# Two copies of the dt rows, and the dt projections in pairs on different row groups

## What is computed

```python
xz = xseq @ in_proj_w.T                 # 384 -> 2 x 768
xin, z = jnp.split(xz, 2, axis=-1)
u = silu(depthwise_conv(xin, taps=3) + conv_b)
dbc = u @ x_proj_w.T                    # 768 -> 24 (dt) + 16 (B) + 16 (C)
dt, Bm, Cm = dbc[..., :24], dbc[..., 24:40], dbc[..., 40:]
dt = softplus(dt @ dt_proj_w.T + dt_proj_b)   # 24 -> 768
A = -exp(A_log)                         # 768 x 16
# for each position t, 768 channels x 16 states:
h = exp(dt_t[..., None] * A) * h + (dt_t * u_t)[..., None] * B_t
y_t = sum_n(h * C_t)
y = (y + u * D) * silu(z)
return y @ out_proj_w.T
```

## Time and profile before

| | |
|---|---|
| Time, median of 3 runs | 3674.62 us (3673.96 to 3679.95) |
| Profiled execution, first to last instruction | 3674.1 us, 50128 instructions |
| Mixer | from 0 to about 2600 us, 16 chunks |
| Two chunks in the steady part | 328 us |
| TensorE's granted clock, mean | 0.969 of full speed |
| DMA, share of the span | 18.6% on the main queue |

### The profile page before, as it was taken

One profiled execution on the slowest core, in us unless ns is written; L12 is line 12 of the kernel. 1 busy time (PEld: TensorE's weight loads), 2 busy tenths in 40 slices (PEclk: granted clock), 3 DMA queues, 4 the chain that ended last, 5 costly groups with the idle time before them and its releaser, 6 DMA issues. The chain is left out here.

```text
span 3674.1 us, 50128 instructions
## 1 busy us (share of the span) xinstructions
PE 3352.4 (91%) x16962; PEld 2370.5 (65%) x16962; DVE 3256.0 (89%) x3376; ACT 2759.3 (75%) x5350; POOL 2577.3 (70%) x2045
## 2 busy tenths in 40 slices
PE   6989989899999989899989989898889998889997
PEld 3666666666666666666666666666657776557776
DVE  3999999999999999999999999999967887876886
ACT  5888797888789788977978787888655554875553
POOL 3898988989898988989898988989921111551100
PEclk7999999999999999999999999999999999999998
DMA  3020211202020211202020210202111113641212
GB/s 134 10 92 19 92 38 65 85 18 85 19 92 19 92 47 55 84 18 85 19 98 23 83 69 33 84 19 85 63 58 35 53 53 143 236 184 40 70 36 87
DMA packets 83586, 249.89 MB, mean 68 GB/s; under 512 B 15212, under 2 KB 24044, under 8 KB 73092
## 3 DMA queue, kind: packets, MB, share of 16 engines
q1 hardware_dynamic: 82564, 245.65, 18.6%
q10 hardware_dynamic: 768, 1.05, 0.1%
HBM read 204.73 MB, written 41.95 MB: 67 GB/s over the span
## 5 line engine op out<-in xcount | busy, mean ns | idle before, releaser
L956 POOL TENSOR_TENSOR slot<-dtu,b_rep 128x512 f32<-128x512 f32 x960 | 1206.4, 1277 | 78.5 <-PE ysum L454 77.8
L966 POOL TENSOR_TENSOR slot<-slot,c_rep 128x512 f32<-128x512 f32 x768 | 974.1, 1278 | 157.3 <-ACT carry L763 92.5
L454 PE MATMUL ysum<-ident,slot 128*128 128x128 f32 x6144 | 831.4, 280 | 31.9 <-POOL slot L966 16.7
L454 PEld LDWEIGHTS ysum<-ident,slot 128*128 128x128 f32 x6144 | 725.9, 145 | 173.0 <-issue 103.1
L754 ACT ACTIVATE state<-dt,aneg 128x512 f32<-128x512 f32 x960 | 655.4, 688 | 237.9 <-DVE slot L1065 200.8
L1065 DVE TENSOR_TENSOR slot<-state,c_rep 128x512 f32<-128x512 f32 x768 | 514.3, 672 | 0.0
L572 PEld LDWEIGHTS state<-diag_b,dtu_t 128*128 128x128 f32 x3072 | 385.0, 194 | 130.3 <-issue 121.1
L572 PE MATMUL state<-diag_b,dtu_t 128*128 128x128 f32 x3072 | 422.7, 281 | 33.0 <-ACT carry L763 16.6
L745 ACT ACTIVATE slot<-dt,aneg 128x512 f32<-128x512 f32 x576 | 405.4, 711 | 23.1 <-PE ysum L454 23.0
L1057 DVE TENSOR_TENSOR_SCAN slot<-state,slot 128x512 f32<-128x512 f32 x288 | 343.3, 1209 | 44.1 <-ACT state L754 33.6
L1057 DVE TENSOR_TENSOR_SCAN slot<-state,carry,slot 128x512 f32<-128x512 f32 x288 | 360.6, 1269 | 6.3 <-POOL slot L956 3.3
(11 more groups left out here) (272 smaller groups left out, 6291.9 us busy)
## 6 DMA issues: line engine op xcount, KB each, us to landing
c_rep<-rows_of_b_and_c SPq DMA_DIRECT2D x64, 1024.0 KB, 5.1
xres_l<-between_layers SPq DMA_DIRECT2D x18, 1536.0 KB, 9.8
xn_l<-between_layers SPq DMA_DIRECT2D x13, 1536.0 KB, 7.1
b_rep<-rows_of_b_and_c SPq DMA_DIRECT2D x16, 1024.0 KB, 4.5
between_layers<-y SPq DMA_DIRECT2D x10, 1536.0 KB, 6.4
xn<-in_x SPq DMA_DIRECT2D x16, 768.0 KB, 4.5
b_rep<-rows_of_b_and_c SPq DMA_DIRECT2D x16, 768.0 KB, 4.1
xres<-in_x SPq DMA_DIRECT2D x16, 768.0 KB, 4.5
```

The lines of the kernel that those rows point to most:

```text
L454: last = mm(ysum[:, cols], slot[:, (NS * k + n) % SLOTS, cols], ident[:], start=first and j == 0, stop=final, is_transpose=True, skip_grou ...
L956: tt(slot[:, q % SLOTS], dtu[:, k % 2], b_rep[:, b_row(n)], ALU.mult).then_inc(dbu_done, 1)
L966: tt(slot[:, q % SLOTS], slot[:, q % SLOTS], c_rep[:, n], ALU.mult).then_inc(pool_mult_done, 1)
```

## The change

The dt columns of `w_x` are loaded twice, to columns 0 to 23 and 64 to 87, and so are the dt weights, to partitions 0 to 23 and 64 to 87 of `w_dt`. The x projection then has 88 output rows instead of 64, and dt lies in rows 0 to 23 and again in 64 to 87. Odd tiles' projections read the second copy, so that two neighbouring ones are on different rows of the array. Tile 0's projection moves from step 57 to step 59, next to tile 1's, and tile 2's from step 63 to 65, next to tile 3's. Steps of all other work stay.

```diff
+DT_ROWS = (0, 64)
+XALL = DT_ROWS[1] + DTR
...
-DT_AT, DT_IN = (57, 59, 63, 65, 2, 18), (BX, BY, BZ, BX, BZ, BZ)
+DT_AT, DT_IN = (59, 59, 65, 65, 2, 18), (BX, BY, BZ, BX, BZ, BZ)
...
-        w_x = sb("w_x", [P, KT, XROWS])
-        w_dt = sb("w_dt", [DTR, DI])
+        w_x = sb("w_x", [P, KT, XALL])
+        w_dt = sb("w_dt", [XALL, DI])
...
-            sp.dma_start(w_x[:, :, XBC:], xw[:, :, DTR:]).then_inc(x_w_in, 16)
-            sp.dma_start(w_x[:, :, 0:DTR], xw[:, :, 0:DTR]).then_inc(x_w_in, 16)
-            sp.dma_start(w_dt[:], dt_wT).then_inc(dt_w_in, 16)
+            sp.dma_start(w_x[:, :, XBC:XROWS], xw[:, :, DTR:]).then_inc(x_w_in, 16)
+            for row in DT_ROWS:
+                sp.dma_start(w_x[:, :, row:row + DTR], xw[:, :, 0:DTR]).then_inc(x_w_in, 16)
+                sp.dma_start(w_dt[row:row + DTR], dt_wT).then_inc(dt_w_in, 16)
...
-                    last = mm(pz[0:XROWS, :], w_x[:, k], u[h][:, k], start=k == 0, stop=k == KT - 1)
+                    last = mm(pz[0:XALL, :], w_x[:, k], u[h][:, k], start=k == 0, stop=k == KT - 1)
...
-                mm(pg[DT_IN[m]][:], w_dt[:, m * P:(m + 1) * P], xp[0:DTR, :], start=True, stop=True).then_inc(dt_full, 1)
+                rows = slice(DT_ROWS[m % 2], DT_ROWS[m % 2] + DTR)
+                mm(pg[DT_IN[m]][:], w_dt[rows, m * P:(m + 1) * P], xp[rows, :], start=True, stop=True).then_inc(dt_full, 1)
...
-            pe.wait_ge(x_w_in, 32)
+            pe.wait_ge(x_w_in, 48)
...
-            pe.wait_ge(dt_w_in, 16)
+            pe.wait_ge(dt_w_in, 32)
...
-                af(xp[0:XROWS, :], pz[0:XROWS, :], ACT.Copy).then_inc(xp_read, 1)
+                af(xp[0:XALL, :], pz[0:XALL, :], ACT.Copy).then_inc(xp_read, 1)
```

## The result

The changed kernel takes 3706.97 us, the median of 4 runs (3705.07 to 3710.62), beside 3675.8 us for the kernel before, timed with it. The ratio is 1.0081, with a 95% interval of 1.0067 to 1.0095: slower, and by more than the forecast of 1.0045. The forecast was 3691 us in a range of 3676 to 3706 us. 1.0081 times the 3674.62 us of its base is 3704.4 us, at the top of that range; the median as measured lies 1 us above it.

A forecast was written before the change was run, and what follows sets the result against it. No engine is full over the span; in the mixer the limit passes from engine to engine, so delays pass on. 8 x 1.8 + 7 x 0.15 + 1 = 16.5 us on 3674.6 gave 3691 us, range 3676 to 3706.

The forecast's parts named there:

- Tile 0's read: ScalarE's read of tile 0's dt projection at step 63, image-starting chunk: at 1167.03 instead of 1164.09, 2.9 us later.
- The gate projection's start: TensorE's gate projection needing tile 1's bank, image-starting chunk: has to wait from 1170.76 to about 1172.6.
- GpSimd's multiplication: GpSimd's multiplication by C of step 64: its carry from ScalarE ready at 1175.55 instead of 1173.75, 1.8 us late.
- The carry's 1.8 us per image-starting chunk: GpSimd waits for ScalarE's late carry of step 64 and stays late: 1.8 us in each of 8 chunks, bounds 1.8 and 2.05.
- the clock: TensorE dropping from 2.4 to 1.2 GHz behind longer waits before two gate projections: 1 us taken, bounds 0 and 14.
- rival C: Clock lost at both longer TensorE waits in most image-starting chunks: 3704 us, up to 3710; chance 0.14.
- The forecast proper: Delay of ScalarE's tile 0 read passed on through the mixer: 3683 to 3698 us around 3691; chance 0.65.
- The other parity: Chunks in an image's second half: slack absorbs most of the delay, 0.15 us each for 7 chunks, bounds 0 and 0.6.
- The second pair: Tile 2's projection moved from step 63 to 65 beside tile 3's: read at step 73, eight steps cover it, 0 us.
- The overlap of a pair: Two neighbouring dt projections on TensorE: half overlap, 0.43 us per pair, bounds nothing and 0.86; in no path term.
- rival A: Freed TensorE time sets the end: at most 35 us gained, to 3640, or 3653 with half the overlap; chance 0.08.
- rival B: VectorE's 2.1 us of idle time takes up ScalarE's delay: 3674.6 plus 0 to 5 us; chance 0.13.

The follow-up runs named there:

- the smaller dose: Kernel before the change with only tile 0's dt projection moved, from step 57 to step 58; 3685.13 us, ratio 1.0019.

## Why the prediction was right, and what it sized wrongly

- **The direction and the first half of the mechanism held, step by step.** Tile 0's read was put at 1167.03 and is at 1179.48 - 12.51 = 1166.97. The gate projection's start was put at 1172.6: 1172.45. GpSimd's multiplication was put at 1175.55: 1175.58. The move alone gives the whole loss and the copies alone none.
- **The carry's 1.8 us per image-starting chunk held**: 1.83 in the changed kernel, and a chunk of 166.0 us in the kernel with the later gate projection where no clock drop comes on top. Eight of these are 14.6 us, against 14.4 in the sum.
- **The mis-sized term is the clock**, which was taken as 1 us between bounds of 0 and 14, with no reason given for a choice near the lower one. From the first scan of each chunk to that of the next, the eight image-starting chunks take 25.3 us longer in the profile. 10.7 us are thus above the carry's part. The clock is down at the fifth gate projection in all eight. This alone costs 0.66 us at the slot (0.34 in the mixer's first chunk), and such chunks take 166.7 to 166.9 us. The first two and the last also have it down at the sixth and take 168.1 to 168.4. The prediction named the wait ahead of the fifth (2.1 us, measured 2.74) and priced a drop at up to 1.8. The wait is longer than it said because the pair overlaps whole and TensorE gets there sooner.
- **The number fell to rival C, not to the forecast.** The forecast proper was 3683 to 3698 us, at a chance of 0.65. 3704.4 is outside it and is the figure of rival C, the clock lost at both waits (chance 0.14). That the range holds it is due to this rival. And C's figure is in part luck: it has 14 us for drops at both waits in most chunks, and the drops cost 10.7, with both in three of eight; the other parity makes up the rest.
- **The other parity** (a chunk in an image's second half) was put at 0.15 us per chunk, 1 us in all; it is 4.2 in all, 0.1 to 1.5 each. The expected chain is there: the read of tile 0 is 2.54 us after ScalarE is ready, and VectorE waits 0.39 for the decay of step 66. The one of 1.5 us is the only one of the seven with the clock down at its sixth gate projection. What spreads the others was not tried.
- **The second pair** was put at 0. The kernel with tiles 0 and 1 alone came out at 1.0062. Its wait ahead of the sixth gate projection is 1.80 us, as before the change, and 2.10 with the second pair; its image-starting chunks take 164.8 to 167.0 us, and none has the clock down there. The intervals of the two kernels just overlap, so this share is seen in the profiles and not shown by the times.
- **The overlap of a pair** was taken as half a projection, since only the inner two of four matmuls were to meet. It is a whole one, 0.85 us: the two projections' matmuls start side by side, both the first ones and both the second ones. It lay in no term of the path. That TensorE's saving is worth nothing (rival A) is shown by the kernel with tiles 2 and 3 alone, 1.0005.
- **Absorption (rival B)** did not occur: each hand-over passed the delay on. Only the first 1.0 us is free: a hole of 1.47 us in ScalarE's queue makes GpSimd wait 0.49 for the carry in the smaller dose, and one of 2.80 makes it 1.83 late here.
- **Left open**: the mixer's first scan starts 1.2 us earlier than before (70.24 against 71.4 us), and the part behind the mixer takes 0.6 us longer. That the clock drops make the 10.7 us rests on comparing chunks of the same kernel with and without one, in several kernels, and not on a version of the changed kernel in which they were taken away. Why the clock falls in one chunk and not in the next was not tried.

## What to carry to other kernels

Moving work later on one engine to group it has to be checked against the in-order reader of its first result, not against the busy share of the engine that is relieved: here 0.3 us of switching and 0.85 us of matmul per pair were won on TensorE, and a 2.8 us hole was made in ScalarE's queue. Where TensorE is made to wait some 2 us, count the work right behind that wait at half its speed as a second price. In these profiles it was paid in some chunks and not in others. It came to 0.7 to 2.3 us in a chunk where scans waited for that work, and to nothing where TensorE's next wait took it up. And before moving a piece of filler work, ask what wait it covers.

## What the runs showed of the hardware

- Two float32 products on rows 0 to 23 and 64 to 87 start 6 to 7 ns apart, in both of their two matmuls, and a pair takes 1.06 us where two on one row group take 1.91. The Trainium skill ("TensorE: Matmul & The Clock Gate", Part 3, the mechanism) gives starts about 4 ns apart and concurrent running. The trace agrees on running together and has starts a little further apart. Whether the ends keep program order it can't show, since the ends of matmuls are modelled.
- After a TensorE wait of the same 2.10 us, for the same ScalarE read, the clock is down in one chunk and not in another of the same kernel: granted 0.79 and 1.00 over 8 us in the kernel with the later gate projection, and in the smaller dose six matmuls in 4.37 us and in 2.68 with 1.3 us between the chunks' lengths. Behind waits of 1.90 and 1.91 us it was down too, in some chunks. At the sixth gate projection it was up in all eight image-starting chunks of the kernel before, where the wait is 1.80 us at most.
